# One transformer decoder block on one Trainium2 core: the score products of the last attention in four portions, one behind each value projection

## What is computed

```python
# x: (8, 512, 256); the FFN stage takes it as S = 8, B = 512, D = 256, H = 4 heads
def _mha(x, Wqkv, bqkv, Wo, bo):
    S, B, _ = x.shape
    hd = D // H
    qkv = x @ Wqkv.T + bqkv
    q, k, v = jnp.split(qkv, 3, axis=-1)
    to_heads = lambda t: t.reshape(S, B, H, hd).transpose(1, 2, 0, 3)
    q, k, v = (to_heads(q), to_heads(k), to_heads(v))
    scores = jnp.einsum('bhqd,bhkd->bhqk', q, k) * (1.0 / np.sqrt(hd))
    att = jax.nn.softmax(scores, axis=-1)
    o = jnp.einsum('bhqk,bhkd->bhqd', att, v)
    o = o.transpose(2, 0, 1, 3).reshape(S, B, D)
    return o @ Wo.T + bo
y = _layer_norm(x + _mha(x, Wqkv, bqkv, Wo, bo), g1, be1)
z = _layer_norm(y + _moe(y, Wg, W1, b1, W2, b2), g2, be2)   # each row goes through one of 8 experts
```

## Time and profile before

| | |
|---|---|
| median of three runs | 1214.45 us (1211.98 to 1217.58) |
| profiled execution | 1213.34 us |
| its span | 1211.3 us |
| PE busy | 1112.3 us (92%) |
| PE weight loads busy | 753.3 us (62%) |
| DVE busy | 734.5 us (61%) |
| ACT busy | 478.9 us (40%) |
| POOL busy | 510.3 us (42%) |

### The profile page before, as it was taken

How to read it: one execution, slowest core, us unless ns; L and a number is a source line. 1 busy time by engine, 2 the same in 40 slices (tenths; PEclk the granted TensorE clock), 3 DMA queues, 4 the chain that set the end, 5 groups by cost and what they waited for, 6 DMA issues and landing times. The chain is left out here.

```text
span 1211.3 us, 29502 instructions
## 1 busy us (share of the span) xinstructions
PE 1112.3 (92%) x10067; PEld 753.3 (62%) x10068; DVE 734.5 (61%) x2088; ACT 478.9 (40%) x866; POOL 510.3 (42%) x758
## 2 busy tenths in 40 slices
PE   8998899999999999999988889998879999999995
PEld 3545455464464554645554446656548999999994
DVE  4554676657756667576536436666574556566563
ACT  5444545454544545444452233233203333333330
POOL 3324425235244252442522022445363665556654
PEclk9999999999999999999999989889989999999998
DMA  7256563735546546336363113537213111111110
GB/s 220 71 155 166 147 188 106 201 102 144 154 116 173 155 112 189 102 106 189 105 182 88 56 36 98 183 107 273 78 51 93 50 49 50 49 51 56 50 44 7
DMA packets 143477, 137.95 MB, mean 114 GB/s; under 512 B 30376, under 2 KB 136750, under 8 KB 143280
## 3 DMA queue, kind: packets, MB, share of 16 engines
q1 hardware_dynamic: 137808, 124.20, 36.0%
q0 software_dynamic: 5280, 12.66, 3.2%
q10 hardware_dynamic: 320, 0.16, 0.1%
HBM read 49.38 MB, written 50.83 MB: 83 GB/s over the span
## 5 line engine op out<-in xcount | busy, mean ns | idle before, releaser
L970 ACT ACTIVATE probs<-ps_ab 128x512 f32<-128x512 f32 (+2 forms) x352 | 174.5, 537 | 95.3 <-PE ps_ab L1292 39.4
L591 POOL TENSOR_SCALAR_AFFINE_SELECT probs<-probs 128x512 f32<-128x512 f32 x128 | 81.7, 638 | 271.1 <-ACT probs L970 267.4
L2854 PE MATMUL ps_ab<-e_yT,e_w_now 128*128 128x128 f32 x1248 | 146.6, 276 | 0.0
L2854 PEld LDWEIGHTS ps_ab<-e_yT,e_w_now 128*128 128x128 f32 x1248 | 143.3, 193 | 0.5 <-ACT e_yT L2825 0.4
L2865 PE MATMUL ps_c<-keep_w,e_hT 128*128 x624 | 141.0, 379 | 0.0
L2865 PEld LDWEIGHTS ps_c<-keep_w,e_hT 128*128 128x128 f32 x624 | 115.7, 190 | 14.1
L712 DVE CUSTOM_DVE_ANT_0 ps_ab<-ps_ab,mask_qk 128x256 f32<-128x256 f32 x224 | 89.0, 451 | 18.8 <-PE ps_ab L1261 18.7
L1822 ACT ACTIVATE e_w_now<-keep_w 128x1024 f32 x78 | 78.2, 1049 | 40.1 <-issue 40.1
L706 DVE TENSOR_REDUCE top<-ps_ab 128x2 f32<-128x512 f32 (+1 forms) x112 | 74.2, 684 | 28.8 <-PE ps_ab L1261 28.0
L2789 DVE TENSOR_SCALAR e_hT<-ps_ab,keep_b 128x128 f32<-128x128 f32 x312 | 84.4, 343 | 8.5 <-PE ps_ab L2854 6.0
L1261 PE MATMUL ps_ab<-k_rows,q_rows 96*128 96x256 bf16 (+1 forms) x512 | 84.5, 260 | 4.6 <-DVE top L712 2.7
(11 more groups left out here) (250 smaller groups left out, 2137.6 us busy)
## 6 DMA issues: line engine op xcount, KB each, us to landing
sorted_rows<-filler SPq DMA_DIRECT2D x8, 4290.0 KB, 17.3
q_rows<-parts SPq DMA_DIRECT2D x96, 128.0 KB, 2.4
k_rows<-parts SPq DMA_DIRECT2D x96, 128.0 KB, 2.4
q_rows<-q_parts SPq DMA_DIRECT2D x96, 128.0 KB, 2.4
keep_w<-in_e_w SPq DMA_DIRECT2D x16, 512.0 KB
keep_w<-in_e_w SPq DMA_DIRECT2D x8, 1024.0 KB
e_row<-sorted_rows SPq DMA_DIRECT2D x39, 130.0 KB, 2.1
x_in<-in_x SPq DMA_DIRECT2D x8, 512.0 KB, 3.9
```

Source lines behind the costliest of these rows:

```text
L591: nc.gpsimd.affine_select(own, own, [[0, TILES], [1, P]], ALU.is_ge, keep_zero, base=0, channel_multiplier=-1).then_inc(probs_cut.sem, 1)
L970: nc.scalar.activation(probs[:, user % 2, lo:lo + width], ps_exp[:, f % 2, 0:width], ACT.Exp).then_inc(exp_done.sem, 1)
L2854: mm = nc.tensor.matmul(ps_h[s][:, f // 4, (f % 4) * P:(f % 4 + 1) * P], w1_now[:, s, k, f * P:(f + 1) * P], yT[:, s, k * P:(k + 1) * P], ...
```

## The change

`scores` is split into `score_masks` (the waits and the two mask matmuls) and `score_blocks(n, c)` (the 16 products of row tile c). In rounds 0 to 6 the masks and the first portion stand behind the first value tile, and each further portion behind one more value tile. The opening (`scores(0)`) keeps its order. The instructions and their operands are the same.

```diff
-                def projected_values(n):
-                    for c in range(TILES):
+                def projected_values(n, tiles=range(TILES)):
+                    for c in tiles:
                         ps = work_claim(pe, n, f"v{c}")
...
                 def scores(n):
 
+                    score_masks(n)
+                    for c in range(TILES):
+                        score_blocks(n, c)
+
+                def score_masks(n):
+
                     pe.wait_ge(q_ready.sem, q_ready.count(n, KD))
                     pe.wait_ge(k_ready.sem, k_ready.count(n, KD))
...
+                def score_blocks(n, c):
+
+                    for tile in range(KD):
+                        block = QUAD * (KD * c + tile)
...
+                    if c == TILES - 1:
+                        mm.then_inc(scores_full.sem, 1)
...
                     if project:
-                        projected_values(n)
-                        scores(n + 1)
+                        projected_values(n, (0,))
+                        score_masks(n + 1)
+                        for c in range(TILES):
+                            score_blocks(n + 1, c)
+                            if c < TILES - 1:
+                                projected_values(n, (c + 1,))
```

More of the change, by code:

```diff
@@ L2519, in scores @@
                                          start=True, stop=False, skip_group_check=True)
[L2520 to L2530, removed]
+                def score_blocks(n, c):
+                    for tile in range(KD):
+                        block = QUAD * (KD * c + tile)
+                        for odd in range(2):
+                            dims = slice(MD * odd, MD * (odd + 1))
+                            for r in range(QUADS):
+                                own = slice(c * P + QUAD * r, c * P + QUAD * (r + 1))
+                                mm = nc.tensor.matmul(ps_scores[QUAD * r:QUAD * (r + 1), odd, block:block + QUAD],
+                                                      qT[dims, tile, own], kT[dims, tile, own],
+                                                      start=False, stop=True, skip_group_check=True)
+                    if c == TILES - 1:
+                        mm.then_inc(scores_full.sem, 1)
                 def heads(n):
```

## The result

Nine runs of each kernel gave medians of 1216.74 us before and **1222.49 us** after (1219.94 to 1226.48), a ratio of 1.0059 with a 95% interval of 1.0044 to 1.0074. The change makes the kernel 0.6% slower, just beyond the 0.5% that a measurement can tell, 5.7 us above the forecast of 1216.8 and 0.5 us outside the range. The profiled execution was the longest of the nine, 1226.48 us with a span of 1224.5 (before 1213.34 and 1211.3), so the two traces show the difference enlarged: 13.2 us of span. I measured it between the first heads of mixing and the last: 160.56 us after, 150.09 before, so 10.5 us lie in the seven rounds, 1.0 ahead of them and 1.7 behind.

What follows compares the result with a forecast made beforehand. PE's instruction supply, slowed by POOL's scatters, was taken to bound rounds 2 to 6. Rounds 0 and 1 +1.2, paused rounds +1.8, last value tile +0.5: +3.5 us on 1213.34 gives 1216.8 us, range 1197 to 1222.

Steps and rivals of the forecast that it cites:

- What bounds the round: Rounds 2 to 6: POOL's scatters slow PE's instructions, costing 13.5 us of pauses and 6.4 of low clock; DVE not bounding.
- Borders: Three times a round a full-width value tile follows small products: 0.2 us each, 0.6 us a round.
- term of 1.2 us for rounds 0 and 1: Rounds 0 and 1 have no pauses, so all added border time is on PE's path: +1.2 us.
- The paused rounds: Rounds 2 to 6: stored instructions carry portion 0 and, except in round 6, portion 1; pause in portion 2, scores end at 9.9.
- rival of the emptier store: Supply already slow at 2.7 us after the heads, two pauses in rounds 2 to 6: +7.7 us, 1221, chance 0.20.
- The term of +1.8 us: Scores' ends in rounds 2 to 6 change by -0.2, 0, +0.2, +0.4 and +1.4 us.
- The clock: Low clock in features and output behind rounds 2 to 5: the 6.4 us stay, as the pause is about as long.
- Round 6 and the last value tile: Round 6 pauses in portion 1, ends at 9.9, +1.4 us; ACT taking the last value tile later adds +0.5 us overall.
- Queue of 64 or store of 76: Instructions held ahead of PE: 76 taken; with 64, portion 2 lasts until the recovery, sum 3.3 us higher, 1220.
- a stretch of time from 5.75 us after the heads on: Form of the slower rival: PE crawls then regardless of any store, third value tile comes behind it, 1218.5.
- The pauses go: Rival: portions fit the refilled store, no pauses in rounds 2 to 6, needing 38 instructions a us: -15.2 us, 1198, chance 0.22.
- Nothing moves: Rival: DVE or the xT1 bank paces the round after all, so time stays; within other cases' 0.03.

Runs made afterwards that it cites:

- third set: Kernel before (1218.23 us) beside itself, the changed kernel (1.0051), the order of before with scatters moved (0.987), and that with scores after two value tiles (0.9861), on another chip.
- sixth set: Kernel before (1218.58 us) beside the changed kernel (1.0079), the changed kernel with scatters 1.5 us later (1.0064), and the order of before with scatters moved (0.988).
- fourth experiment: Kernel before with value tiles 0 to 2, masks, score portion 0, value tile 3, then portions 1 to 3, scatters in place: 1217.31 us, 1.0001.
- fifth set: Kernel before (1203.14 us) beside itself (1.0006), the changed kernel (0.9972), and the changed kernel with scatters 1.5 us later (0.9971).
- second and fourth set: Kernel before (1206.06 and 1205.65 us) beside, in one, three kernels with scores at other places; in the other, the changed kernel with scatters 1.5 us later (0.9978).
- first and second set: Kernel before (1217.44 and 1206.06 us) beside edits of scatters and order in one, and of the scores' place in the other.
- first experiment: Order of before on PE, POOL's four scatters moved to the head of the next round, against the kernel before: 1198.34 us, 0.984.
- second experiment: Changed kernel with the scatters moved to the head of POOL's next round, against the kernel before: 1201.16 us, 0.9857.
- fifth experiment: Kernel before with masks and all scores right behind the heads, ahead of the value tiles, scatters in place: 1219.05 us, 1.0113.

## Why the prediction was wrong

**What bounds the round: right.** The pauses are the scatters' doing; moving them takes away all handfuls and 19 us, where 13.5 + 6.4 had been read from the earlier trace rows. DVE is at most a small part of it: the edit that starts it earlier on top of that gained nothing in the third set. That edit does take PE's wait for the bank of xT1 away, and its round 2 is 0.3 us shorter from heads to heads (19.45 us against 19.77), but it has single pauses of 1.76 and 2.39 us in rounds 3 and 5.

**Borders: mis-sized.** 0.2 us each was taken; they cost 0.107 (7.13 against 6.81 for three), the lower bound that the earlier trace rows gave. The Trainium skill's page "TensorE: Matmul & The Clock Gate", section "LDWEIGHTS (loading the stationary operand)", gives the same 107 ns for the weight load of 128 columns. The term of 1.2 us for rounds 0 and 1 measured 0.7.

**The paused rounds: the step that failed.** It read "The scatters begin at 770.31 - 767.12 = 3.2" and let the supply be quick until then, so that portion 0 would leave a full store and the first pause fall into portion 2. The pause stands in portion 1. In round 3, 64 + 8 + 30 = 102 instructions went through from the start of portion 0 at 798.68 to the first pause at 800.33. A store of 76 with 14 a microsecond over those 1.65 us makes 99. So store and rate fit, but the supply must have been slow at 798.68 already, 0.09 us ahead of the scatter's own row at 798.77; in the sixth set, with later scatters, the same sum from portion 1's start (799.95, 0.22 ahead of the scatter) makes 101 where 110 went through. POOL's row is preceded by 0.65 us of "issue", and the work that slows PE may well begin in it; that is an argument from the place alone. In round 2 the scatter begins 0.44 us after portion 0 does, and 130 instructions went through before the pause, so there the store was partly refilled, and still the pause came in portion 1. Part of the step is a plain misreading: 3.2 is round 2's figure. In the kernel before the first scatter of rounds 3 to 5 begins 2.93, 3.09 and 2.99 us after the heads, in the changed one 2.81, 3.15 and 2.98, and portion 0 runs from 2.7 to 3.0, in round 4 to 3.4. Between the two there was at most 0.2 us in which the store could fill again.

For rounds 2 to 5 this is the rival of the emptier store, which had 0.20 and 1221. It put the ends of rounds 2 to 6 at 10.9, 10.5, 10.4, 10.4 and 9.9; they are 11.8, 12.8, 12.6, 11.6 and 9.7, 6.3 us more than it in sum in the profiled execution. Most of what it lacked stands in the windows: the value tiles behind the pause run partly or wholly at 1.2 GHz. In round 3 they take 1.85 and 1.52 us instead of 1.09 each, at granted clocks of 0.50 and 0.70, and over rounds 2 to 5 six such tiles are 5.2 us longer than 1.09 each. It lacked also that the handfuls get thinner: from 800.33 to 804.2 the trace has 17 matmul records in round 3, some 9 instructions a microsecond with their loads.

**The term of +1.8 us** for rounds 2 to 6 came to +10.8 in the profiled execution. Of the whole sum, +3.5, the medians show +5.75 and the ratio, applied to 1216.74, +7.2; the profiled pair overstates it.

**The clock: half right.** The stretches behind the rounds are 2.30, 0.08, 0.07 and 2.56 us longer than 5.66, 5.0 in all where 6.4 were to stay. But a low clock inside rounds 2 to 5, on value tiles, had no term. It was placed only behind the scores, since before there was nothing but scores at that place.

**Round 6 and the last value tile.** Round 6 does pause early, in portion 0, but that pause isn't the emptied store's: with the scatters moved away it stands at the same product, 0.46 us long, and beside them it takes 1.18. The prediction had no term for such single pauses; the last section has them. The round has no low stretch, its later tiles take 1.09 us. The 0.5 us for ACT's last value tile is of the right size in round 1: the features start 0.26 us after the ranks, right behind ACT's row, where it was 0.21, and with a wait for the bank of xT1 of 0.97 us for 0.90 the heads of rounds 1 and 2 lie 0.45 us further apart, 0.13 more than the borders.

**Queue of 64 or store of 76.** By the opening table of the Trainium skill's page "TensorE: Matmul & The Clock Gate", 64 instructions, the sum was some 3.3 us higher, 1220, nearer to the result, but for another reason. The rows still speak for 76: with 64, 88 instructions should have gone through in the fourth experiment, where 104 did. The rule of the Trainium skill's page "Runtime: NRT & Kernel Launch", section "Instruction fetch mechanics", that fetching is normally hidden, is not borne out in these rounds. Nor is what the prediction made of it, a stretch of time from 5.75 us after the heads on: in rounds 2 to 5 of the changed kernel the first pause begins at 4.4 to 4.8 us. It comes no fixed time after the scatter either: 3.0 and 3.9 us after the first scatter's row in rounds 2 and 6 of the kernel before, each time within a microsecond of the first scores, and 1.6 us after it in rounds 2 and 3 of the changed one.

**"The pauses go".** In the fifth set the supply is 38 a microsecond beside the scatters of round 2, just what this rival asked for (the kernel before takes 1206 us in the second and fourth set too), and the changed kernel is then faster, but by 0.3%, not the 15 us that the rival counted: in such a set the kernel before has little to give back, its rounds 0 to 6 ending 7.2 us over 6.81 each instead of 13.5, and the changed one has its single pauses. **"Nothing moves"** is untrue in either.

So the sign of this change hangs on the set. In the three measurements where the kernel before takes 1217 to 1219 us it is 0.5 to 0.8% slower; in the one where it takes 1203, 0.3% faster, and its version with later scatters, which is no faster than it where both were timed, was 0.2 to 0.3% faster in two such sets. What makes the sets differ is **open**. It is not the chip alone, since the first and second set ran on one chip; the program, its scatters and their durations are the same.

The best version of either kernel is the order of before with the scatters at the head of POOL's next round: 0.984, 0.987 and 0.988 in three sets of the longer kind. It was not run in a set of the shorter kind; its variant with the scores in the middle had 0.9941 there.

## What to carry to other kernels

Dense runs of tiny products behaved here as if they lived on a store of instructions that must be refilled: where PE's timeline shows handfuls of one size with idle time put down to "issue", look at what GpSimd is issuing beside them, and move that before reordering PE. If the order on PE is changed all the same, put every long product ahead of the place where the supply fails; what is left behind it costs its whole time, and here, in part, at half the clock. Repeat a difference under 1% beside the old kernel in several sets before the sign is believed.

## What the runs showed of the hardware that I had not expected

**Two rates.** While POOL runs the same indirect DMAs, PE's instructions come at about 14 a microsecond in some sets and at 38 or more in the fifth, and the same kernel takes 1217 to 1219 or 1203 to 1206 us.

**Pauses every 256 instructions.** PE's timeline of the first experiment, round 3, has two pauses in which no scatter runs:

```profile
787.30 1.30 PE L2545 MATMUL ps_ab<-m_probsT,m_v 32*64 32x32 f32 x106
788.76 0.43 PE L2545 MATMUL ps_ab<-m_probsT,m_v 32*64 32x32 f32 x22 [0.16 <-issue]
789.12 3.83 PE L2481 MATMUL ps_d<-m_w_qkv,e_w_now 128*128 128x264 f32 x16
792.78 0.38 PE L2518 MATMUL ps_c<-m_mask_pos,m_ident 128*128 128x256 bf16 x2
793.09 0.96 PE L2527 MATMUL ps_c<-e_w_now 64*32 64x32 f32 x88
795.31 0.56 PE L2527 MATMUL ps_c<-e_w_now 64*32 64x32 f32 x40 [1.27 <-issue]
```

Between them lie 22 + 16 + 2 + 88 = 128 matmuls and as many loads, 256 instructions. The Trainium skill's page "Runtime: NRT & Kernel Launch", section "Instruction fetch mechanics", says that instructions are fetched in blocks of 256 and that the cost of a border is mostly hidden. The spacing agrees. So do the other single pauses: from one to the next the second experiment has 379, 380 and 251 matmuls, the fifth 380 and 251 in turn, with their loads 8 to 10 short of 3 and 2 times 256, as if a few instructions that the profile does not list stood between. The borders that do not show fall into long products or small gaps. Hidden they are not where they show, with 1.27 us here and 1.93 us in round 0 of the fifth experiment. Where a border falls depends on every instruction ahead of it, so a change in the order or the number of instructions can move the time by a microsecond or two. The change of this document does so: in rounds 4 and 6 a border that cannot be seen in the first experiment stops portion 0 in the second.

**A small VectorE add beside a scatter.** DVE's groups by line, 705 to 880 us, first of the kernel before, then of the first experiment (count, busy us, mean ns):

```profile
L2226 DVE TENSOR_TENSOR m_xnb<-m_v,m_gate_sums 128x32 f32<-128x32 f32 x8 | 5.4, 677 | 0.0
```

```profile
L2226 DVE TENSOR_TENSOR m_xnb<-m_v,m_gate_sums 128x32 f32<-128x32 f32 x8 | 12.5, 1568 | 0.0
```

Beside the moved scatters this 128x32 addition takes up to 3.19 us; in the kernel before it took 0.15 to 0.86. The scores of the first experiment still come 6.6 to 7.0 us after the heads in the rounds without a pause, so it did not pace them; it is the price of the new place.
